# A routing stage with its scores in column lanes and its scatters spread out, and its last shared down product in the program that follows

## The chip, the cores and the metric

One NeuronCore of a Trainium2 chip runs the whole program as one launch. The metric is the device time in microseconds (us), the median of three runs. Two layers of a transformer-like network are computed on two sequences of 2048 tokens of 256 features; all of it is in float32. The change lies in the feed-forward part of the first layer, a mixture of experts.

## The reference, cut to what matters

```python
# layer 0, second half; x is [2 * 2048, 256]; h = layernorm(x) * (1 + cb) + sb
scores = h @ router                        # 256 x 8
topv, topi = top_k(scores, 2)
gates = sigmoid(scores, -inf where not chosen)
routed_e = h * gates[:, e]                 # each chosen token, times its gate
out_e = (silu(routed_e @ w_in[e]) * (routed_e @ w_swiglu[e])) @ w_out[e]
shared = (silu(h @ w_in_shared.T) * (h @ w_swiglu_shared.T)) @ w_out_shared.T
x = x + gb * (shared + sum_e out_e)
```

## The kernel before, in words

The part is two programs, one after the other, each a block in which every engine has its own hand-written order of instructions; engines wait for each other by semaphores alone. All engines of one program must have ended before any starts the next.

**route_tokens** (line 879) walks over four blocks of tokens, `it` = 0 to 3. A block is 512 tokens of each of the two sequences (`b` = 0, 1), so 1024 tokens, or eight tiles of 128. TensorE computes the shared expert for all tokens: eight projections `up(it, q)`, each into one of two buffers `ps[:, q % 2]`; ScalarE makes the silu, VectorE's `product(it, q)` multiplies and so frees the buffer for `up` two later. `down(it, b)` is the second product of the shared expert; for `b` = 1 it is made in the next block, after `up(it + 1, 1)`. VectorE scales its result (`output`), and GpSimd adds it to `x` (`add_output`); for the last block VectorE adds.

In between lies the routing. `turn` transposes the normalised rows of the next block after `up` 2 to 5. `scores(it + 1)` (line 1243) follows `down(it, 0)`: for each of eight tiles the 128 x 128 piece of `hT` is the stationary operand and the 128 x 8 router is moved through. VectorE finds the two best (`best`), marks them (`choose`: a cast, two comparisons and a sum), TensorE counts the places (`ranks`, after `up(it, 1)`), VectorE turns them to rows of a table in HBM (`place_rows`) and multiplies the tokens by their gates (`gate_rows`). GpSimd issues sixteen indirect DMAs (`scatter`) in a row that write the gated rows to HBM, and then makes four tensor operations for the next block (`modulate`: scale and shift of the rows of both sequences).

`product(it, 7)` stands behind `choose(it + 1)` in VectorE's order, and `up(it + 1, 1)` waits for `product(it, 7)`; this couples VectorE's routing work to TensorE.

**run_experts** (line 1316) takes 71 blocks of 128 rows of the table. For a block, SyncE loads the rows, TensorE transposes them (`turn`), ScalarE and VectorE copy the weights of the block's expert to a buffer (`fetch_in`, `fetch_sw`), TensorE makes `up` and `down`, and the result is stored. Its second weights, `w_out` of eight experts and of the shared one (4.7 MB), are loaded at the start by nine DMAs from GpSimd's queue (line 1358), and `down(0, 0)` waits for all of them. TensorE begins with sixteen transposes that compute nothing (`spin`), then `turn` 0 and 1, then `up` 0.

## Time and profile before

| | |
|---|---|
| median of the runs | 3204.3 us (3202.83 to 3207.18) |
| the profiled execution | 3175.27 us, of which the span of the trace is 3173.4 us |
| mean granted TensorE clock in it | 0.989 |
| TensorE matmuls, busy | 3053.4 us (96%) |
| VectorE, ScalarE, GpSimd, busy | 1954.9, 1721.0, 763.4 us |
| route_tokens on TensorE | 503 to 714 us of the span |
| run_experts on TensorE | 717 to about 1123 us |

A row of the timeline has the start in us, the time from there to the end of its last instruction, the engine, the line and operation, output and inputs, the shape of an array tile for TensorE and of the operands, the number of instructions, and in brackets the idle time ahead of it with what ended that. A float32 matmul shows as two records, each a pass of its own.

### The profile page before, as it was taken

The page shows a single profiled execution, that of the slowest core. Times are in us where ns is not written, and L with a number is a line of the kernel's source. Part 1 is how long each engine was busy: PE and PEld are TensorE (multiplying, and loading weights), DVE is VectorE, ACT ScalarE, POOL GpSimd, SP SyncE. Part 2 cuts the span into 40 slices and gives each one's busy share as a digit, 9 for nine tenths or more (in the row PEclk, how much of TensorE's full clock was granted, in tenths as well). Part 3 has the DMA queues.
Part 4 walks back from the last instruction along what each step waited for, and adds up shares of the span by engine and source line. Part 5 has one row for each costly group of instructions (what it writes and reads, how often), then busy time and mean ns, then how long its engine had stood idle before and what let it go on. Part 6 is the DMA issues. An engine that isn't in the chain of part 4 may idle for free. (4 is left out here: it accounts for less than half of the span.)

```text
span 3173.4 us, 49527 instructions
## 1 busy us (share of the span) xinstructions
PE 3053.4 (96%) x16616; PEld 1908.5 (60%) x16617; DVE 1954.9 (62%) x4607; ACT 1721.0 (54%) x3801; POOL 763.4 (24%) x1037
## 2 busy tenths in 40 slices
PE   8999998998999989999998999999999999998999
PEld 4455556558999963333334666665555666666555
DVE  6999995653333346666664787785333777777342
ACT  6776762213333326665665888875222777776221
POOL 1111113550000035555533222221011112112111
PEclk9999999999999999999999999999999999999999
DMA  9900004013111121111101000000001000000000
GB/s 330 318 1 1 1 1 165 29 54 103 46 48 48 45 77 29 31 29 26 29 14 42 10 11 9 10 8 32 1 0 36 9 11 10 9 9 5 14 14 27
DMA packets 114255, 134.11 MB, mean 42 GB/s; under 512 B 14478, under 2 KB 100342, under 8 KB 113786
## 3 DMA queue, kind: packets, MB, share of 16 engines
q1 hardware_dynamic: 106042, 109.54, 10.6%
q0 software_dynamic: 7872, 21.77, 2.2%
q8 instruction: 117, 1.92, 0.3%
q14 instruction: 96, 0.79, 0.1%
q10 hardware_dynamic: 128, 0.10, 0.0%
HBM read 60.30 MB, written 60.83 MB: 38 GB/s over the span
## 5 line engine op out<-in xcount | busy, mean ns | idle before, releaser
L1880 DVE CUSTOM_DVE_ANT_0 sb_win_masked<-ps_win_pss,sb_win_around 128x384 f32<-128x384 f32 (+1 forms) x512 | 256.3, 538 | 167.0 <-PE ps_win_pss L2008 166.9
L2320 ACT ACTIVATE sb_loc_pr<-ps_loc_psw,sb_loc_nb,sb_loc_sc 128x256 f32<-128x256 f32 x512 | 281.0, 569 | 135.9 <-DVE sb_loc_nb L2465 135.9
L2547 PE MATMUL ps_stk_banks<-sb_stk_w,sb_loc_hT 128*128 128x512 f32 x768 | 348.3, 603 | 2.7 <-ACT sb_loc_hT L2287 2.7
L1742 ACT ACTIVATE sb_win_pT<-ps_win_pst 128x512 f32<-128x512 f32 x368 | 199.8, 596 | 167.3 <-PE ps_win_pst L2019 167.2
L1473 PE MATMUL ps_exp_ps<-sb_exp_xT,sb_exp_here 128*128 128x128 f32 x2272 | 266.8, 276 | 0.0
L1473 PEld LDWEIGHTS ps_exp_ps<-sb_exp_xT,sb_exp_here 128*128 128x128 f32 x2272 | 261.0, 193 | 0.1
L2008 PE MATMUL ps_win_pss<-sb_win_kT,sb_win_q 32*128 32x384 f32 (+1 forms) x1024 | 230.4, 520 | 31.7 <-DVE sb_win_qtok L1880 21.3
L2547 PEld LDWEIGHTS ps_stk_banks<-sb_stk_w,sb_loc_hT 128*128 128x128 f32 x768 | 141.2, 190 | 177.9 <-issue 177.9
L752 PE MATMUL ps_rec_psp<-sb_rec_hT,sb_rec_w 128*128 128x512 f32 x512 | 230.1, 592 | 0.8 <-DVE sb_keep_modf L543 0.8
L2842 DVE SCALAR_TENSOR_TENSOR sb_mlp_hid<-ps_stk_banks,sb_stk_col,sb_mlp_gl 128x512 f32<-128x512 f32 (+1 forms) x112 | 75.1, 672 | 245.5 <-ACT sb_mlp_gl L2797 245.3
L2019 PE MATMUL ps_win_pst<-sb_win_qm,sb_win_kT 32*128 32x512 f32 x736 | 211.2, 647 | 1.5 <-ACT sb_win_pT L1742 1.5
L1665 POOL TENSOR_SCALAR_AFFINE_SELECT sb_win_pT<-sb_win_pT 128x512 f32<-128x512 f32 x240 | 146.5, 634 | 244.3 <-ACT sb_win_pT L1742 244.3
L2233 POOL TENSOR_TENSOR sb_loc_t<-sb_loc_t 128x512 f32<-128x512 f32 x64 | 81.4, 1272 | 468.1 <-DVE sb_loc_t L2411 468.0
L2008 PEld LDWEIGHTS ps_win_pss<-sb_win_kT,sb_win_q 32*128 32x128 f32 x1024 | 81.7, 183 | 161.2 <-DVE sb_win_qtok L1880 148.8
L2461 DVE TENSOR_REDUCE sb_loc_top<-ps_loc_psw 128x4 f32<-128x1024 f32 x128 | 156.1, 1219 | 24.9 <-PE ps_loc_psw L2585 22.4
L752 PEld LDWEIGHTS ps_rec_psp<-sb_rec_hT,sb_rec_w 128*128 128x128 f32 x512 | 96.3, 190 | 116.5 <-issue 116.5
L1637 POOL DMA_INDIRECT sb_win_got<-expert_results,sb_keep_row x64 | 61.9, 968 | 416.5 <-POOLq L1353 401.4
L2900 PE MATMUL ps_mlp_pso<-sb_stk_w,sb_mlp_hid 128*128 128x256 f32 (+1 forms) x768 | 160.5, 383 | 0.0
L1426 DVE TENSOR_TENSOR sb_exp_hid<-ps_exp_ps,sb_exp_act_f 128x512 f32<-128x512 f32 x71 | 49.1, 692 | 169.0 <-PE ps_exp_ps L1473 169.0
L2797 ACT ACTIVATE sb_mlp_gl<-ps_stk_banks,sb_stk_col 128x512 f32<-128x512 f32 x48 | 33.0, 687 | 217.1 <-PE ps_stk_banks L2889 217.0
L2900 PEld LDWEIGHTS ps_mlp_pso<-sb_stk_w,sb_mlp_hid 128*128 128x128 f32 (+1 forms) x768 | 133.1, 189 | 28.6 <-issue 10.5
L1393 ACT COPY sb_exp_xT<-ps_exp_psx 128x256 f32<-128x256 f32 x71 | 26.4, 372 | 223.8 <-PE ps_exp_psx L1464 223.8
(362 smaller groups left out, 6725.2 us busy)
## 6 DMA issues: line engine op xcount, KB each, us to landing
sorted_tokens<-sb_rec_blank SPq DMA_DIRECT2D x9, 4224.0 KB, 30.2
sb_exp_rows<-sorted_tokens SPq DMA_DIRECT2D x71, 128.0 KB, 2.0
expert_results<-sb_exp_res SPq DMA_DIRECT2D x71, 128.0 KB, 1.7
sb_moe_w_in<-in_L_ffn_w_in_eDF SPq DMA_DIRECT2D x8, 512.0 KB, 10.7
sb_moe_w_sw<-in_L_ffn_w_swiglu_eDF SPq DMA_DIRECT2D x8, 512.0 KB, 10.8
sb_exp_w_out<-in_L_ffn_w_out_eFD POOLq DMA_DIRECT2D x8, 512.0 KB, 8.7
sb_stk_angles<-in_angles SPq DMA_DIRECT2D x32, 128.0 KB, 3.8
sb_stk_xs_b<-sb_stk_y SPq DMA_DIRECT2D x64, 63.5 KB
```

What stands on the lines that cost most here:

```text
L752: i = nc.tensor.matmul(out, w[:, k, j * REC + g * P:j * REC + (g + 1) * P], hT[:, G % 2, k], start=(k == 0), stop=(k == KD - 1))
L1473: i = nc.tensor.matmul(ps[:, k % 2, j, f * P:(f + 1) * P], here[:, k % 2, j, c * FF + f * P:c * FF + (f + 1) * P], xT[:, k % 2, c], start= ...
L1665: nc.gpsimd.affine_select(part, part, [[0, AG], [-towards, P]], ALU.is_ge, outside, base=0, channel_multiplier=towards).then_inc(s_cut, 1)
L1742: nc.scalar.activation(pT[:, n % PARTS], pst[:, n % TURNED], ACT.Exp, scale=SC).then_inc(s_e, 1)
L1880: nc.vector.tensor_tensor_reduce(masked[:, pair % 2, j, 0:keys], pss[:, (n + j) % PLAIN, 0:keys], around[:, first:first + keys], 1.0, -3e3 ...
L2008: nc.tensor.matmul(pss[:, n % PLAIN, 0:len(keys) * P], q[rows, u % RINGS, g], kT[rows, keys[0]:keys[-1] + 1].rearrange("p a n -> p (a n)") ...
L2019: nc.tensor.matmul(pst[:, n % TURNED], kT[rows, key], qm[rows, u % 2].rearrange("p g n -> p (g n)"), start=True, stop=True, skip_group_che ...
L2233: nc.gpsimd.tensor_tensor(qq, qq, t2[:, 0:INNER], ALU.add).then_inc(s_rope, 1)
L2320: e = nc.scalar.activation(pr[:, hf, h], psw[:, hf, h // 2, h % 2 * 256:h % 2 * 256 + 256], ACT.Exp, scale=sc8[:, b, hh:hh + 1], bias=nb[: ...
L2461: nc.vector.tensor_reduce(top[:, hf], psw[:, hf].rearrange("p a (h n) -> p (a h) n", h=2), AX_X, ALU.max).then_inc(s_top, 1)
L2547: t = nc.tensor.matmul(psa[:, c], hT[:, b, k, 1 - k:P + 1 - k], w[:, k, c * 512:(c + 1) * 512], start=(k == 0), stop=(k == KD - 1))
L2900: i = nc.tensor.matmul(pso[:, t], hid[at:at + M, b, f, t * P:(t + 1) * P], w2[at:at + M, f], start=(f == 0 and t % 2 == 0), stop=(f == KH ...
```

## The change

The scores of a block are computed the other way round: the router, padded from 8 to 32 columns, is the stationary operand, and 256 tokens at a time are moved through; the four groups of 256 tokens use the four groups of 32 columns of the array and so 32 partitions each of one bank (`LANE`, `scores`). ScalarE copies the bank (`copy_lanes`), and two transposes (`turn_scores`) give the layout that `best` reads. The instructions lie inside `down(it, 0)`: the scores after its second quarter, the transposes after its last. `down` waits for each quarter of `hid` by itself. `ranks` comes after `up(it, 0)` instead of `up(it, 1)` (after `up(0, 2)` in the first block), and the gates on ScalarE after `silu` 0. On VectorE `place_rows` comes before `product` 1 and both `gate_rows` come before the output of the block before. In the first block `up(0, 0)` goes ahead of the transposes of the scores, and the scores no longer wait for `ones` and `before`. GpSimd's scatters go in four groups of four DMAs, and the scale, shift and add operations stand between them.

`down(3, 1)` with its scaling and addition moves from the end of route_tokens to run_experts, where it takes the place of `spin`; `hid`, `og`, the shared `w_out` and the PSUM tile are allocated across both for it. VectorE scales and adds after its first two weight copies. `up(0, 0)` there goes ahead of `turn(0, 1)`, and `silu(0, 0)` ahead of the second copy of rows. VectorE no longer waits at the end of route_tokens for the scatters to have landed; SyncE waits for them in run_experts before its first load of rows.

```diff
@@ route_tokens, GpSimd: modulate() is split in scale(it, b) and offset(it, b), scatter(it) in settle_rows(it) and scatter(pair)
                 for it in range(NBLK):
+                    settle_rows(it)
+                    scatter(0)
                     if it:
                         add_output(it - 1, 1)
-                    scatter(it)
+                    scatter(1)
                     if it + 1 < NBLK:
-                        modulate(it + 1)
+                        scale(it + 1, 0)
+                    scatter(2)
+                    if it + 1 < NBLK:
+                        offset(it + 1, 0)
+                    scatter(3)
+                    if it + 1 < NBLK:
+                        scale(it + 1, 1)
+                        offset(it + 1, 1)
                         add_output(it, 0)
@@ route_tokens, ScalarE
+                def copy_lanes(it):
+                    act.wait_ge(s_lanes, it + 1)
+                    nc.scalar.copy(lane_scores[:], psg[:, 0:2 * P]).then_inc(s_lanes_here, 1)
...
-                        if it and q == 1:
+                        if q == 0:
                             nc.scalar.preload_act_table_set(LN_SET)
                             gates(it)
@@ route_tokens, VectorE
+                product(0, 0)
                 best(0)
                 choose(0)
                 weigh(0)
+                product(0, 1)
+                for b in range(NB):
+                    scale_rows(1, b)
+                product(0, 2)
+                place_rows(0)
+                for b in range(NB):
+                    gate_rows(0, b)
 
                 for it in range(NBLK):
                     ahead = it + 1 < NBLK
-                    product(it, 0)
-                    product(it, 1)
                     if it:
+                        product(it, 0)
                         weigh(it)
-                    place_rows(it)
-                    if ahead:
+                        place_rows(it)
+                        product(it, 1)
                         for b in range(NB):
-                            scale_rows(it + 1, b)
-                    if it:
+                            gate_rows(it, b)
+                        if ahead:
+                            for b in range(NB):
+                                scale_rows(it + 1, b)
                         output(it - 1, 1)
-                    gate_rows(it, 0)
-                    product(it, 2)
-                    gate_rows(it, 1)
+                        if not ahead:
+                            table_ends()
+                        product(it, 2)
                     product(it, 3)
...
-                output(NBLK - 1, 1)
-                add_output(NBLK - 1, 1)
-                dve.wait_ge(s_sorted, NBLK * ROUTED * 16)
@@ route_tokens, TensorE
-                    for b in range(NB):
-                        pe.wait_ge(norm.s_hT, norm.ready(it, b))
-                        for n in range(TB):
-                            at = (b * TB + n) * EXP
-                            for k in range(KD):
-                                i = nc.tensor.matmul(psg[:, at:at + EXP], hT[:, it % 2, b, k, n * P:(n + 1) * P],
-                                                     router[:, k], start=(k == 0), stop=(k == KD - 1))
+                    pe.wait_ge(norm.s_hT, norm.ready(it, NB - 1))
+                    for k in range(KD):
+                        for lane in range(P // LANE):
+                            b, half = lane // HALVES, lane % HALVES
+                            i = nc.tensor.matmul(psg[lane * LANE:(lane + 1) * LANE, 0:2 * P], router[:, k],
+                                                 hT[:, it % 2, b, k, half * 2 * P:(half + 1) * 2 * P], start=(k == 0),
+                                                 stop=(k == KD - 1), skip_group_check=True)
+                    i.then_inc(s_lanes, 1)
+
+                def turn_scores(it):
+                    pe.wait_ge(s_lanes_here, it + 1)
+                    for j in range(HALVES):
+                        i = nc.tensor.transpose(psg[:, (2 + j) * P:(3 + j) * P], lane_scores[:, j * P:(j + 1) * P], ident[:])
                     i.then_inc(s_score, 1)
...
                     for f in range(KF):
+                        pe.wait_ge(s_hid, it * UF + b * KF + f + 1)
...
+                        if b == 0 and it + 1 < NBLK:
+                            if f == 1:
+                                scores(it + 1)
+                            if f == KF - 1:
+                                turn_scores(it + 1)
...
                 pe.wait_ge(s_w, 16 * 5)
+                scores(0)
+                pe.wait_ge(s_shared, 16 * 3)
+                up(0, 0)
+                turn_scores(0)
                 pe.wait_ge(s_ones, 1)
                 pe.wait_ge(s_b, 16)
-                scores(0)
-                pe.wait_ge(s_shared, 16 * 3)
                 for it in range(NBLK):
                     for q in range(UF):
-                        up(it, q)
-                        if q == 1:
+                        if it or q:
+                            up(it, q)
+                        if q == (0 if it else 2):
                             ranks(it)
-                            if it:
-                                down(it - 1, 1)
+                        if it and q == 1:
+                            down(it - 1, 1)
...
-                down(NBLK - 1, 1)
@@ run_experts, SyncE, VectorE, TensorE
+                sp.wait_ge(s_sorted, NB * NBLK * TB * 2 * 16)
                 for n in range(UNROLL):
                     load(0, n)
...
                 fetch_sw(0, 0)
                 fetch_sw(0, 1)
+                late_output()
                 product(0, 0)
...
-                spin(nc, ident, psw, 16)
+                for f in range(KF):
+                    late_down(f)
                 turn(0, 0)
+                up(0, 0)
                 turn(0, 1)
-                up(0, 0)
```

## Rows read from the trace of the kernel before

**Rows 1.** The page, busy time of each engine over the span.
```profile
PE 3053.4 (96%) x16616; PEld 1908.5 (60%) x16617; DVE 1954.9 (62%) x4607; ACT 1721.0 (54%) x3801; POOL 763.4 (24%) x1037
```
**Rows 2.** Waits of TensorE, 500 to 720: total us, times, longest.
```profile
PE ps_route_ps L1260 <- DVE sb_route_hid L1166: 7.4, 3, 3.9
```
**Rows 3.** Timeline, start of route_tokens.
```profile
506.48 0.47 SPq L949 DMA_DIRECT2D sb_route_w_out<-in_shared_out  x1
...
510.07 5.38 PE L1250 MATMUL ps_route_psg<-sb_route_router,sb_route_hT 128*128 128x8 f32 x32 [2.40 <-issue]
...
515.30 3.62 PE L1260 MATMUL ps_route_ps<-sb_route_hT,sb_moe_w_in 128*128 128x512 f32 x4
```
**Rows 4.** DMA issues, 500 to 740: count, KB, median us to landing.
```profile
sb_route_w_out<-in_shared_out SPq DMA_DIRECT2D x1, 512.0 KB, 6.4
sb_exp_w_out<-in_shared_out POOLq DMA_DIRECT2D x1, 512.0 KB, 13.1
```
**Rows 5.** Timeline of TensorE, scores(1) and the projections behind them.
```profile
547.37 3.63 PE L1250 MATMUL ps_route_psg<-sb_route_router,sb_route_hT 128*128 128x8 f32 x32
550.86 1.96 PE L1260 MATMUL ps_route_ps<-sb_route_hT,sb_moe_w_in 128*128 128x512 f32 x4
...
554.37 1.88 PE L1260 MATMUL ps_route_ps<-sb_route_hT,sb_moe_w_in 128*128 128x512 f32 x4
```
**Rows 6.** Timeline of TensorE: up(1, 1), ranks(1), and up(1, 6) behind scores(2).
```profile
565.33 2.73 PE L1260 MATMUL ps_route_ps<-sb_route_hT,sb_moe_w_in 128*128 128x512 f32 x4 [3.92 <-DVE sb_route_hid L1166]
...
570.56 0.19 PE L1267 MATMUL ps_route_psg<-sb_route_chosen,sb_route_before 128*128 128x64 bf16 x1
...
603.85 3.66 PE L1260 MATMUL ps_route_ps<-sb_route_hT,sb_moe_w_in 128*128 128x512 f32 x4
```
**Rows 7.** Windows, TensorE: stretch, length, busy, granted clock, DMA share, GB/s.
```profile
565.30:568.70 3.40, 3.37 (x5) 0.67 0.00 0
603.80:607.20 3.40, 3.40 (x6) 0.53 0.22 78
```
**Rows 8.** Timeline of VectorE, the two comparisons of choose(0) and of choose(1).
```profile
517.88 0.36 DVE L1118 TENSOR_TENSOR sb_route_pick<-sb_route_number,sb_route_topf 128x64 f32<-128x64 f32 x2
...
557.53 4.72 DVE L1118 TENSOR_TENSOR sb_route_pick<-sb_route_number,sb_route_topf 128x64 f32<-128x64 f32 x2
```
**Rows 9.** Timeline of GpSimd: block 0's last scatter, a scale, the slowest scatter.
```profile
554.09 0.96 POOL L976 DMA_INDIRECT sorted_tokens<-sb_route_gated,sb_route_rowu  x1 [0.30 <-issue]
...
559.82 2.35 POOL L964 TENSOR_TENSOR sb_route_xn<-sb_route_xn,sb_layer_moe_scale_row 128x1024 f32<-128x1024 f32 x1
...
700.61 1.44 POOL L976 DMA_INDIRECT sorted_tokens<-sb_route_gated,sb_route_rowu  x1 [0.30 <-issue]
```
**Rows 10.** Timeline of TensorE, four products in 32-column tiles in a later stage.
```profile
1186.08 1.06 PE L2044 MATMUL ps_win_pso<-sb_win_pT,sb_win_v 128*32 128x512 f32 x8
```
**Rows 11.** Timeline, end of route_tokens.
```profile
706.16 0.69 DVE L1166 TENSOR_TENSOR sb_route_hid<-ps_route_ps,sb_route_act_f 128x512 f32<-128x512 f32 x1 [2.74 <-ACT sb_route_act_f L1013]
...
706.91 7.17 PE L1285 MATMUL ps_route_pso<-sb_route_w_out,sb_route_hid 128*128 128x256 f32 x32 [1.41 <-DVE sb_route_hid L1166]
...
715.38 1.22 DVE L1179 TENSOR_TENSOR sb_keep_x<-sb_keep_x,sb_route_og 128x1024 f32<-128x1024 f32 x1
```
**Rows 12.** Timeline, start of run_experts.
```profile
717.25 3.29 PE L116 MATMUL ps_exp_psw<-sb_keep_ident 128*128 128x128 f32 x16 [3.16 <-PEq L939]
...
722.71 0.44 PE L1464 MATMUL ps_exp_psx<-sb_keep_ident,sb_exp_rows 128*128 128x128 f32 x2 [2.18 <-DMA sb_exp_rows<-sorted_tokens]
...
723.81 0.75 POOL L1358 DMA_DIRECT2D sb_exp_w_out<-in_shared_out  x1
726.64 0.69 PE L1464 MATMUL ps_exp_psx<-sb_keep_ident,sb_exp_rows 128*128 128x128 f32 x2 [3.49 <-DMA sb_exp_rows<-sorted_tokens]
...
732.41 3.74 PE L1473 MATMUL ps_exp_ps<-sb_exp_xT,sb_exp_here 128*128 128x128 f32 x32
...
737.09 1.99 PE L1487 MATMUL ps_exp_pso<-sb_exp_w_out,sb_exp_hid 128*128 x8 [0.94 <-DVE sb_exp_hid L1426]
```

105 lines of the change are left out of this document (65 added, 40 removed).

## The prediction, made before the changed kernel was run

> **What bounds the kernel now.** Read the page's busy times first: TensorE works 96% of the span [rows 1], so a change in this stage pays what it takes from TensorE's own line of work, and nothing that it takes from another engine. Then read TensorE's waits in 500 to 720: in all the routing stage it waits for VectorE's product three times, 7.4 us together, the longest 3.9 [rows 2]. Next its timeline: the start, where the scores run from 510.07 and the first projection follows at 515.30 [rows 3]; a block, where the scores take 550.86 - 547.37 = 3.49 us and a projection 554.37 - 550.86 = 3.51 [rows 5] (3.43 where nothing precedes it but another); and the two places where passes run slower: up(1, 1) behind the 3.92 us wait takes 570.56 - 565.33 = 5.23 us, and the first four passes of up(1, 6), straight behind the scores, 3.66 instead of 1.88 [rows 6]. The windows show why: the granted clock was 0.67 and 0.53 there [rows 7], a stretch with time at the lower level, 1.2 instead of 2.4 GHz. Before the one the engine was idle for 3.92 us; before the other it made the thirty-two narrow passes. Last, the end: the last projection's product begins at 706.16, the last down product at 706.91, and two operations of VectorE end the program at 715.38 + 1.22 = 716.6 [rows 11]; the experts' program starts at 717.25, gets its first rows at 722.71 and its second at 726.64, and makes its first down product at 737.09 [rows 12].
>
> **The change, part by part.** All sums are made against the profiled execution (3175.27 us), which is 29.0 us below the median of the runs; I take the difference between the kernels to be the same in both.
>
> *Start.* up(0, 0) no longer follows the old scores. It waits for three shared weights; the last of them is issued at 506.48 and takes 6.4 us to land [rows 3, 4], so 512.9. The new scores lie ahead of that: they start after the affine of the rows, near 509, and are 16 passes. So the first projection starts at 512.9 instead of 515.30: 2.4 us. The cost of its first half at the lower clock (3.62 us for four passes [rows 3]) stays.
>
> *Scores of blocks 1 to 3.* Sixteen passes of 256 columns in four column tiles replace thirty-two. The nearest row is of the same tile shape: eight passes of 512 columns in 1.06 us [rows 10], so four tiles do work side by side. Counted by columns the new ones take 1.0 us, counted by passes 2.1; without any overlap 3.4 (a projection's pass of 512 columns takes 3.43 / 8 = 0.43 us, one of 256 half of it, sixteen times). I take 1.5, since the row is of this form, and 0.3 for the two transposes, below the 0.44 that two take with their end [rows 12]. ScalarE's copy between them hides under two quarters of the down product (3.5 us). So 3.49 - 1.8 = 1.7 us a block, 5.1 in three; the bounds are a loss of 0.6 (three times 3.4 + 0.3 against 3.49) and a gain of 6.6 (1.0 + 0.3).
>
> Eight passes of 0.43 us on four tiles would take 0.86; the row shows 1.06 [rows 10], so 0.2 us is all that entering and leaving the narrow tiles can have cost there. The Trainium skill (TensorEngine Tiling (Array Packing), Key Properties) says that changing the tiling mode drains TensorE; by that rule each scoring inside a down product pays two such changes, which at 0.2 us for each is 1.2 us in three blocks off the sum; it moves no rival.
>
> *TensorE's waits for product(it, 7).* VectorE's two comparisons take 0.36 us in choose(0), but 4.72 in choose(1), when GpSimd runs its scale and shift, 2.35 us each [rows 8, 9]: each comparison ends with a GpSimd operation. I put the whole of the 7.4 us down to that. In the new order the scores are ready at the end of down(it, 0), 3.5 us earlier, and ranks ask for `chosen` after up(it, 0), 3.4 us earlier; the two cancel. What moves is GpSimd: gate_rows now start after product 1 and end 14 us into a block (up(it, 0) 3.4, silu and two table loads to 8.9, two times 2.2), so its queue runs from 14.5: sixteen scatters at 0.96 + 0.30 = 1.26 us, 20.2, and six operations of 2.35, 14.1 [rows 9], to 49 in a block of 45.8 (eight projections 27.4, two down products 13.9, turns 1.8, ranks 0.8, scores 1.8). choose runs from 44 and meets the last three operations (42 to 49), so it ends 3.3 into the next block; ranks ask at 3.4, product 7 ends at 4.0, up 1 asks at 4.2. So nothing is left of the wait where the queue starts on time. In block 1 it doesn't: its gate_rows meet the first block's addition and end 2.1 us later; that leaves 1.8 us. Gain 7.4 - 1.8 = 5.6. The bounds: with two more collisions a block (2.35 each) the waits stay as they are, 0; with none, 7.4.
>
> *The lower clock.* If the 3.92 us wait and the thirty-two narrow passes go, so do their costs: 5.23 - 3.43 = 1.8 us and 3.66 - 1.88 = 1.8 us [rows 6, 7]. The wait that I leave, 1.8 us, is nearer to the idle 1.41 us behind which the down product ran at full speed (7.17 us for 32 passes [rows 11]) than to the 3.92. Gain 3.6; bounds 0 and 3.6.
>
> *The turn in block 0.* VectorE's place_rows now follow the scaling of the rows, so the 0.4 us wait of the first turn goes.
>
> *End.* Before, the program ended 716.6 - 706.85 = 9.75 us after the last product of a projection [rows 11]: down(3, 1) and two operations of 1.22 us. They go to run_experts. GpSimd's last scatter is issued 37 us into a block of 42, five before the end; so SyncE's new wait for the scatters, behind which all loads of rows are queued, costs nothing. The price of the moved part: down(0, 0) there waits for nine loads of w_out, the last issued at 723.81, landing 13.1 us later at 736.9 [rows 4, 12]; TensorE was ready at 732.41 + 3.74 = 736.15. So this start is bound by 4.7 MB of weights: 737.09 - 717.25 = 19.8 us from the start. New order on TensorE from its start: 7.0 for the moved product; turn(0, 0), whose rows land at 5.5, 0.4; copy 0.6; up(0, 0) 3.7; turn 1, whose rows land at 9.4, and its copy, 1.2; up(0, 1) 3.7: 16.6 us, 3.2 below 19.8. Even if the moved product's first half ran at the lower clock (3.5 more) the end would move by 0.3 us only. Gone with `spin` is nothing that counts. VectorE's two operations lie between its weight copies and product(0, 0), which waits until 11 us. So all 9.75 us are gained. An idle time of 3.2 us ahead of down(0, 0) may bring the lower clock; a step there costs up to 1.8 us, I take 1.
>
> Sum: 2.4 + 5.1 + 5.6 + 3.6 + 0.4 + 9.75 - 1.0 = 25.9 us. I round down to 25 for small waits of the new order: the profiled execution at 3150.3 us, the median at 3204.3 - 25 = **3179.3 us**.
>
> **The rivals.** *The collisions stay.* For it: every GpSimd operation but one still runs while VectorE casts, compares or scales, and the margins above are a few tenths. Against: only three of the six still lie near choose. Then the waits (5.6) and the wait's clock (1.8) aren't gained: 25 - 7.4 = 17.6, so 3186.7 us. The Trainium skill (SBUF — State Buffer, the diagram's notes on the shared port pair) says that a VectorE operation with two inputs in SBUF and a GpSimd operation that reads SBUF exclude each other, each for its whole length. That is the rule under the 4.72 us; the trace agrees (0.36 against 4.72).
>
> *The experts' start doesn't hide it.* If the weights were not the limit but the rows' loads or TensorE's own order, of the 9.75 us the moved product's 7.0 would come back on TensorE: 25 - 7 = 18, 3186.3 us. Against it stands the landing at 736.9.
>
> *The change does little.* The scores gain nothing (no overlap of the tiles), collisions stay, and the moved product comes back: 25 - 5.7 - 7.4 - 7 = 4.9, so 3199.4 us. It needs all three.
>
> *Slower: GpSimd's queue sets the pace.* From gated(it) over sixteen scatters and six operations to the shift that the next gate_rows wait for is a ring: 14.1 - 2.35 + 20.2 + 4.4 + 1 = 37 us against a block of 45.8. One scatter took 1.44 us instead of 0.96 [rows 9]. VectorE's scaling and statistics now lie beside scatters. From an issue of 1.26 + 8.8 / 16 = 1.8 us the ring decides; at 3.5 us it is 37 + 16 x 2.24 = 73, three blocks cost 3 x 27 = 81 us and the kernel is 81 - 25 = 56 us slower, 3260; it is slower at all from about 2.4 us. Sixty-three of the 64 issues show 0.96 to 1.05 and stood partly beside the same VectorE work.
>
> **How the numbers follow.** The forecast has 0.66, with its own range from 19.3 (tiles without overlap, 5.7 less) to 28 (neither the wait of 1.8 nor the clock's 1.0): 3176 to 3185. Collisions that stay 0.15, an experts' start that doesn't hide it 0.08, both among 3184 to 3189; little 0.07; slower 0.04. The range that should hold 8 in 10 goes from 3174 (28 us and a run-to-run spread of 2) to 3192 (collisions that stay and tiles without overlap, 25 - 7.4 - 5.7 = 12 us). Under 0.2% (6.4 us) a measurement of this kernel can't tell a difference from none; faster by more 0.90, within 0.06, slower 0.04.
>
> **What would show it.** In the changed profile: the first projection at about 513; the scores as 16 passes in 1 to 2 us inside the down product; no wait for product 7 over 2 us, and no window of the stage after 520 with a clock under 0.9; route_tokens ending about 26.5 us earlier on TensorE's start of the experts (717.25 to about 691); down(0, 0) 19.8 us behind that start, with the idle time ahead of it. Wrong would be the sum if VectorE's comparisons again take 4 us with TensorE waiting, if the column tiles run one behind the other, or if down(0, 0) comes later than 20.5 us behind its start.

## The result, and the profile of the changed kernel

The changed kernel took 3166.32 us (median, 3165.41 to 3166.53), the kernel before 3205.16 us (3202.83 to 3207.18): a ratio of 0.9875, 95% interval 0.9859 to 0.989, so 38.8 us less where the forecast was 25 and the range ended at 3174. The two profiled executions tell another size: spans of 3173.4 and 3164.8 us, 8.6 us apart. That contradiction is the real question of this case, and the runs below answer most of it.

First the trace of the changed kernel against the steps of the prediction. Waits of TensorE, 500 to 720, the answer to [rows 2] (total us, times, longest):

```profile
PE ps_exp_pso L1544 <- DMA sb_exp_w_out<-in_shared_out: 4.4, 1, 4.4
PE ps_route_ps L1299 <- DMA sb_moe_shared_out<-in_shared_out: 3.2, 1, 3.2
PE ps_route_psg L1306 <- DVE sb_route_chosen L1151: 2.3, 1, 2.3
...
PE ps_route_pst L1272 <- DVE sb_route_xn L1119: 1.4, 1, 1.4
```

The wait for product 7 is gone; what is left of it is one wait of `ranks` for `chosen` (2.3) and a new one of a turn for rows that VectorE normalises (1.4). TensorE's timeline, where [rows 3], [rows 5] and [rows 6] stood:

```profile
510.15 1.07 PE L1282 MATMUL ps_route_psg<-sb_route_hT,sb_route_router 128*32 128x256 f32 x16 [1.19 <-ACT sb_route_hT L1023]
514.38 3.78 PE L1299 MATMUL ps_route_ps<-sb_route_hT,sb_moe_w_in 128*128 128x512 f32 x4 [3.16 <-DMA sb_moe_shared_out<-in_shared_out]
517.95 3.12 PE L1299 MATMUL ps_route_ps<-sb_route_hT,sb_moe_w_sw 128*128 128x512 f32 x4
...
540.50 3.62 PE L1324 MATMUL ps_moe_pso<-sb_moe_shared_out,sb_route_hid 128*128 128x256 f32 x16
544.05 1.07 PE L1282 MATMUL ps_route_psg<-sb_route_hT,sb_route_router 128*32 128x256 f32 x16
545.05 3.72 PE L1324 MATMUL ps_moe_pso<-sb_moe_shared_out,sb_route_hid 128*128 128x256 f32 x16
548.61 0.38 PE L1290 MATMUL ps_route_psg<-sb_keep_ident,sb_route_lane_scores 128*128 128x128 f32 x2
548.82 1.88 PE L1299 MATMUL ps_route_ps<-sb_route_hT,sb_moe_w_in 128*128 128x512 f32 x4
...
563.05 7.07 PE L1324 MATMUL ps_moe_pso<-sb_moe_shared_out,sb_moe_late_hid 128*128 128x256 f32 x32
569.96 1.88 PE L1299 MATMUL ps_route_ps<-sb_route_hT,sb_moe_w_in 128*128 128x512 f32 x4
...
608.19 0.20 PE L1306 MATMUL ps_route_psg<-sb_route_chosen,sb_route_before 128*128 128x64 bf16 x1 [2.32 <-DVE sb_route_chosen L1151]
```

The scores of a block take 545.05 - 544.05 = 1.00 us and their transposes 548.82 - 548.61 = 0.21. The down product around them takes 3.55 + 3.56 = 7.11 us in its two halves, an undivided one 569.96 - 563.05 = 6.91; so the scores cost 1.00 + 0.21 + 0.20 = 1.41 us a block instead of 3.49. The whole of up(0, 0) ran at the lower clock, 6.53 us (514.38 to 520.91). The windows of TensorE for it, for up(2, 1) behind the wait for `chosen`, and for down(0, 0) of the experts, to be read as [rows 7]:

```profile
514.40:520.90 6.50, 6.50 (x8) 0.53 1.05 407
608.80:612.30 3.50, 3.50 (x5) 0.56 0.00 0
716.00:720.00 4.00, 4.00 (x11) 0.50 0.00 0
```

The end, the answer to [rows 11, 12]:

```profile
691.67 1.88 PE L1299 MATMUL ps_route_ps<-sb_route_hT,sb_moe_w_sw 128*128 128x512 f32 x4
695.23 7.14 PE L1551 MATMUL ps_moe_pso<-sb_moe_shared_out,sb_moe_late_hid 128*128 128x256 f32 x32 [1.68 <-PEq L947]
702.21 0.38 PE L1521 MATMUL ps_exp_psx<-sb_keep_ident,sb_exp_rows 128*128 128x128 f32 x2
...
707.91 3.74 PE L1530 MATMUL ps_exp_ps<-sb_exp_xT,sb_exp_here 128*128 128x128 f32 x32
716.00 3.77 PE L1544 MATMUL ps_exp_pso<-sb_exp_w_out,sb_exp_hid 128*128 x8 [4.36 <-DMA sb_exp_w_out<-in_shared_out]
```

The rows are there when the moved product is done (no wait at 702.21), and down(0, 0) waits for the weights, 20.8 us behind the program's first matmul, as before (19.8). VectorE and GpSimd around that wait for `chosen`, the answer to [rows 8, 9]:

```profile
603.17 4.70 DVE L1147 TENSOR_TENSOR sb_route_pick<-sb_route_number,sb_route_topf 128x64 f32<-128x64 f32 x2
...
603.15 2.34 POOL L976 TENSOR_TENSOR sb_route_xn<-sb_route_xn,sb_layer_moe_shift_row 128x1024 f32<-128x1024 f32 x1
605.46 2.34 POOL L994 TENSOR_TENSOR sb_keep_x<-sb_keep_x,sb_route_og 128x1024 f32<-128x1024 f32 x1
```

The last down product of the experts starts at 1120.51 before and 1102.24 after: 18.3 us, or 19.6 counted from the spin at the start of route_tokens (503.38 and 504.67). So this pair of executions has the gain that the prediction's mechanism gives, less some us, and then loses 11 us of it in the windowed attention (583.7 us before, 594.9 after; another execution of the kernel before has 590.3). It doesn't have 38.8.

### The profile page after: what moved, and what is told of

Its sections match the earlier page's. It is cut to its first block and busy times, and to the rows that moved or that the text cites. A ratio compares the mean times of both kernels' runs of the same rounds, so it can differ in the third digit from the quotient of the medians.

```text
span 3164.8 us, 49386 instructions
## 1 busy us (share of the span) xinstructions
PE 3051.6 (96%) x16544; PEld 1895.5 (60%) x16545; DVE 1947.1 (62%) x4607; ACT 1725.4 (55%) x3807; POOL 764.8 (24%) x1037
## 5 line engine op out<-in xcount | busy, mean ns | idle before, releaser
L2074 PE MATMUL ps_win_pss<-sb_win_kT,sb_win_q 32*128 32x384 f32 (+1 forms) x1024 | 233.9, 528 | 31.2 <-DVE sb_win_qtok L1946 20.5
L2966 PEld LDWEIGHTS ps_mlp_pso<-sb_stk_w,sb_mlp_hid 128*128 128x128 f32 (+1 forms) x768 | 133.1, 189 | 28.6 <-issue 10.5
```

The lines of the kernel that those rows point to most:

```text
L2074: nc.tensor.matmul(pss[:, n % PLAIN, 0:len(keys) * P], q[rows, u % RINGS, g], kT[rows, keys[0]:keys[-1] + 1].rearrange("p a n -> p (a n)") ...
L2966: i = nc.tensor.matmul(pso[:, t], hid[at:at + M, b, f, t * P:(t + 1) * P], w2[at:at + M, f], start=(f == 0 and t % 2 == 0), stop=(f == KH ...
```

## The experiments

Every job shows the kernel before beside its own runs. A chip is named by a number; each job ran on one. In this section "the spin" is the row of transposes on TensorE with which route_tokens begins, the common zero of two traces. "remote" in a row stands where the profile names no engine and no DMA as what ended a wait.

**Both kernels again.** No edit.

> The kernel before, unchanged, on the chip of these runs. My theory: the gain of the routing stage and of the experts' start is 21 us at the experts' first down product (737.09 to 716.0), 18 us at the experts' end; the rest of the difference between the two measured gaps (8.6 us between the profiled executions, 38.8 us between the medians) comes from the windowed attention or a later stage of the kernel before, which has more than one duration. It expects executions of this kernel that differ by up to 29 us with the routing stage alike within 2 us, and the difference all behind 1125 us. The rival: the slower executions are slower in the routing stage itself (collisions of GpSimd and VectorE that fall otherwise), and then the gain there is above 21 us.

> The changed kernel, unchanged, beside it. Theory: 3166 us, all its executions within 2 us of one another, the experts' first down product at 716 us, and the windowed attention from 1107 to about 1702 us. The rival (each kernel has several durations of the later stages by chance of the chip): some execution near 3195 or near 3156.

Chip 14: the kernel before 3178.19 us (19 runs, 3172.28 to 3184.82), itself as an experiment 3176.56 (ratio 0.9993), the changed one 3156.73 (ratio 0.9927, 0.991 to 0.9943): 21.5 us. The changed kernel is 10 us faster than its first time, the kernel before 27 us. So it is mainly the kernel before that has two levels: a first near 3205 to 3209 us, and one near 3178. In the routing its two traces are alike within 2 us, as expected (the last projection starts 200.2 and 198.6 us behind the spin). The executions of the changed kernel, expected within 2 us of 3166, lie from 3152.76 to 3165.53: there the rival held.

**The parts alone.** Routing only puts the old end back:

```diff
-                dve.wait_ge(s_x, (NBLK - 1) * NB)
-                dve.wait_ge(s_last, 1)
+                output(NBLK - 1, 1)
+                add_output(NBLK - 1, 1)
+                dve.wait_ge(s_sorted, NBLK * ROUTED * 16)
+                dve.wait_ge(s_x, (NBLK - 1) * NB)
+                dve.wait_ge(s_last, NB)
...
+                down(NBLK - 1, 1)
```

> The routing change alone; the last down product with scaling and addition stays at the end of route_tokens, and run_experts is as before, with its spin. Theory: the experts' program starts 12 to 14 us earlier than before (near 704), and its first down product comes 19.8 us behind that. If the later stages keep their durations, 12 to 14 us faster than before. The rival, that the windowed attention's duration hangs on when it starts, expects another offset of up to 30 us either way that arises behind the experts.

Late product only is the kernel before with the changed run_experts:

```diff
-                down(NBLK - 1, 1)
...
+                for f in range(KF):
+                    late_down(f)
```

> The moved down product alone, with the new start of run_experts; the routing of the kernel before. Theory: the experts' program starts 9.7 us earlier (near 707.5), its first down product 19.8 to 21 us behind that; 8 to 10 us faster at that place. If the moved product were not hidden there: 2 to 3 us. The rival on the later stages again expects an offset that arises behind the experts.

Chip 14: 3164.15 us (0.995, 0.9934 to 0.9967), 14.0 us less, as expected, and 3175.94 (0.9995, 0.9986 to 1.0005), 2.3 less, which isn't clear of noise, where 8 to 10 were expected. Alone, the moved product gains almost nothing. TensorE and GpSimd of that kernel:

```profile
706.31 0.96 POOL L979 DMA_INDIRECT sorted_tokens<-sb_route_gated,sb_route_rowu  x1 [0.30 <-issue]
...
712.93 9.11 PE L1506 MATMUL ps_moe_pso<-sb_moe_shared_out,sb_moe_late_hid 128*128 128x256 f32 x32 [7.27 <-PEq L942]
...
713.38 6.12 POOL L1358 DMA_DIRECT2D sb_exp_w_out<-in_L_ffn_w_out_eFD  x8 [6.11 <-POOLq L942]
```

GpSimd's last indexed write is done at 707.3, yet the next program starts 5.7 us later on TensorE and 6.1 later on GpSimd. In the changed kernel the last write is issued in full at 688.2, 5.4 us before TensorE is through with the program (693.55), and the start at 695.23 waits for little. So the move pays in full only because the new order has the last write issued before TensorE is done (14.0 + 2.3 against 21.5 together).

**The new scores alone**, in the kernel before.

```diff
-        router = m.sb("router", [P, KD, EXP])
+        router = m.sb("router", [P, KD, LANE])
+        lane_scores = m.sb("lane_scores", [P, 2 * P])
...
                                 scores(it + 1)
+                                turn_scores(it + 1)
```

> The kernel before with the scores in column lanes alone (scores, copy and transposes right behind down(it, 0), all else as before). Theory: the sixteen passes and two transposes take 1.2 us of TensorE instead of 3.5, the copy between them is no longer hidden (about 0.8 us more of waiting), so 1.5 us a block, and the lower clock of up(1, 6), which I put down to the thirty-two narrow passes, is gone (1.8 us). 5 to 6 us earlier at the end of route_tokens; the three waits for product 7 stay at 1 to 4 us each. The rival (the waits for VectorE have the same root as the clock) expects the waits to go too: 12 us.

Chip 11: 3172.85 us against 3178.98 (0.9989, 0.9974 to 1.0005): not clear of noise by the times. In the trace the last projection starts 194.7 us behind the spin, where the kernel before has 200.2 and 198.6 in two traces: about 4 to 5.5 us less. The three waits for product 7 are all there (0.79, 4.19, 4.16 us), so the passes and the waits are separate gains.

**GpSimd's order**, two ways, in the changed kernel: the writes in one row, or the second modulation ahead of the last four writes.

```diff
-                    scatter(0)
+                    for pair in range(4):
+                        scatter(pair)
                     if it:
                         add_output(it - 1, 1)
-                    scatter(1)
...
```

> The changed kernel with GpSimd's sixteen scatters in one row again, its tensor operations behind them (the addition of the block before first). Theory: what counts is only that the last operations of GpSimd meet choose; their end stays 34.3 us behind gated rows, so TensorE's waits stay within 1 us of those of the changed kernel (2.3 us for chosen in block 2, with 1.8 us of lower clock behind it), route_tokens as long within 2 us. The rival, that spreading the scatters is what frees VectorE, expects 5 us or more longer.

```diff
+                        scale(it + 1, 1)
+                        offset(it + 1, 1)
                     scatter(3)
-                    if it + 1 < NBLK:
-                        scale(it + 1, 1)
-                        offset(it + 1, 1)
+                        pool.wait_ge(s_chosen, it + 2)
```

> The changed kernel with GpSimd's three operations of sequence 1 ahead of the last four scatters, and the addition of sequence 0 held until chosen is there. Theory: choose meets no GpSimd operation that holds it for long; comparisons at 0.36 us; the wait for chosen in block 2 (2.3 us) and the lower clock behind it (1.8 us) vanish: route_tokens ends 4 us earlier than in the changed kernel. The rival (the lower clock comes by chance of the moment, not from the wait) expects 2.3 us at most.

**The idle time ahead of the experts' first down product covered**, in the changed kernel.

```diff
+                        pe.wait_ge(s_late_og, 1)
+                        spin(nc, ident, late_pso[:, 0], 34)
                         pe.wait_ge(s_wo, 16 * (EXP + 1))
```

> The changed kernel with 34 transposes that compute nothing between up(0, 1) and down(0, 0) of run_experts, where TensorE waits 4.4 us for the last weights. Theory: the wait is for the weights, so down(0, 0) stays at 20.8 us behind the start, and without an idle time the first down product takes 1.99 instead of 3.77 us and the up behind it 3.74 instead of 4.61: 2.8 us less to the end of the experts. If the weights were not the limit down(0, 0) would come later by the transposes' 3.7 us.

Chip 11: 3152.83 us (0.9909, 0.9889 to 0.9928), 3152.82 (0.9914, 0.9896 to 0.9932) and 3152.4 (0.9914, 0.9897 to 0.9932). The changed kernel itself didn't run on this chip; on two others it took 3156.7 and 3156.6, so the gain of about 4 us is one between jobs. The row of writes was expected to make no difference, and its trace has no wait for `chosen` at all: the last projection starts 181.3 us behind the spin, where the changed kernel has 186.8 to 187.0 in three traces and 183.3 and 183.5 in two others, so 2 to 5.7 us sooner. In the changed kernel it is the interleaving that puts an addition beside VectorE's comparisons. The other order moves the wait (1.61 us, in block 1, at full clock behind it; 182.7). The transposes of the third kernel give down(0, 0) its clock back; the row above them is its wait for `chosen`:

```profile
606.77 0.20 PE L1306 MATMUL ps_route_psg<-sb_route_chosen,sb_route_before 128*128 128x64 bf16 x1 [2.30 <-DVE sb_route_chosen L1151]
...
708.36 3.88 PE L119 MATMUL ps_moe_pso<-sb_keep_ident 128*128 128x128 f32 x34
712.66 1.99 PE L1546 MATMUL ps_exp_pso<-sb_exp_w_out,sb_exp_hid 128*128 x8 [0.42 <-DMA sb_exp_w_out<-in_shared_out]
```

1.99 us instead of 3.77, and from down(0, 0) to the last one 383.4 us instead of 386.2, as the kernel before has it (383.4). It has the same instructions as the changed kernel up to there, and still its last projection came 3.5 us sooner behind the spin (183.5): the waits are alike, 2.30 and 1.42 us, but up(2, 1) ran at full clock, as its window shows:

```profile
607.40:610.90 3.50, 3.50 (x8) 1.00 0.00 0
```

That much two executions of one program differ.

**Both kernels cut short.** Up to here my theory was that the executions of a kernel part only in the windowed attention, with the clock that each is granted there. Leaving stages out tells whether they do. The edit is one line, in both kernels, with stages=(1, 2, 3) for the other pair:

```diff
-    build_program(nc, aps)
+    build_program(nc, aps, stages=(1, 2))
```

> Leaves out the windowed attention and the local layers: the kernel before, cut behind the experts, whose rows are stored and not added (x is written out as the recurrence left it). Last experts' down product of the full kernel before: 1120.5 us of the span, so some 1125 to 1160 us with the stores and the output. Theory (the executions of one kernel part only behind the experts, in the windowed attention, with its granted clock): the executions of this cut kernel lie within 3 us of each other, where those of the full one lie 12 to 17 us apart. Rival (they part in the recurrence, the routing or the experts): they lie apart by more than 6 us, and the granted clock of the stages goes with it.

> Leaves out the windowed attention and the local layers: the changed kernel, cut at the same place. Theory: 18 to 20 us below the cut kernel before (last down product at 1102.2 and 1120.5, with spins at 504.7 and 503.4), executions within 3 us of each other; the forecast's 25 us would need the whole of the end's 9.75 and of the waits. Rival (the 38.8 us of the first measurement are the change's own work): more than 25 us, up to 39.

> Leaves out the local layers: the kernel before cut behind the windowed attention. Spin of that stage at 1125.3 and 583.7 us of windowed attention: near 1715 to 1740 us with the output. Theory: the executions lie 6 to 14 us apart, nearly as far as those of the full kernel (12 to 17), longer where the granted clock is lower. Rival (the local layers spread them): within 3 us.

> Leaves out the local layers: the changed kernel cut behind the windowed attention. Theory: its median 10 to 20 us below the cut kernel before, less exactly than with two stages, since each execution draws its clock in the windowed attention; no fixed share of 39 us. Rival (the earlier end of the experts makes the windowed attention itself shorter for a fixed reason): the difference is over 30 us in every pair of executions.

This job ran on chip 7, where the kernel before took 3207.17 us (3200.03 to 3213.14), so the first level again. Two stages: 1160.33 and 1118.67 us, 41.7 apart where my theory had 18 to 20, executions within 5 us. Three stages: 1754.09 and 1715.01, 39.1 apart. The whole of the 38.8 us lies in the first two stages: there my theory fell and its rival held. Executions do spread more with the windowed attention (8.4 and 10.6 us against 4.9 and 3.2), as the theory said, but the difference of the kernels doesn't arise there. The cut kernel before has what the profile ahead of the prediction does not show. TensorE, scores(2):

```profile
602.12 2.23 PE L1250 MATMUL ps_route_psg<-sb_route_router,sb_route_hT 128*128 128x8 f32 x18
604.68 0.17 PE L1250 MATMUL ps_route_psg<-sb_route_router,sb_route_hT 128*128 128x8 f32 x1 [0.33 <-issue]
606.08 0.40 PE L1250 MATMUL ps_route_psg<-sb_route_router,sb_route_hT 128*128 128x8 f32 x2 [1.23 <-issue]
606.81 0.38 PE L1250 MATMUL ps_route_psg<-sb_route_router,sb_route_hT 128*128 128x8 f32 x1 [0.34 <-issue]
608.90 0.17 PE L1250 MATMUL ps_route_psg<-sb_route_router,sb_route_hT 128*128 128x8 f32 x1 [1.71 <-issue]
...
612.14 3.58 PE L1260 MATMUL ps_route_ps<-sb_route_hT,sb_moe_w_in 128*128 128x512 f32 x4
```

612.14 - 602.12 = 10.0 us for what takes 3.49 in [rows 5]; the other blocks 7.4 and 9.0. No wait on a semaphore explains the gaps ("issue"). In the same time VectorE stands before its scaling of the down product, which TensorE finished at 602.1, and GpSimd issues indexed writes; the rows of both:

```profile
607.50 0.96 POOL L976 DMA_INDIRECT sorted_tokens<-sb_route_gated,sb_route_rowu  x1 [0.30 <-issue]
...
611.10 1.23 DVE L1173 TENSOR_TENSOR sb_route_og<-ps_route_pso,sb_keep_gates 128x1024 f32<-128x1024 f32 x1 [14.80 <-remote]
```

VectorE starts 2.6 us behind the end of the last of sixteen writes, 9 us late (its wait in the kernel's profile ahead of the prediction was 6.0 us, here 14.8). The same comes in all four blocks, at 552.82, 611.10, 664.95 and 717.84: 3.1 us before, 2.6 and 1.2 behind and 0.3 before the end of the last write, after waits of 10.5, 14.8, 13.4 and 8.2 us (6.0, 6.0, 6.0 and 0.6 in the profile ahead of the prediction). What is handed on during the first six writes isn't late: VectorE's product at 591.73 follows right behind ScalarE's end at 591.70. The one at the end holds back the last product: 26.3 us from the last projection to the experts' first turn instead of 19.1, and 10.6 us are lost before it. TensorE of the cut changed kernel on the same chip loses nothing of the kind: its last projection is 187.0 us behind the spin, as in the changed kernel's first profile.

Two smaller marks of it are there all the same. Only in blocks 1 and 2 does the changed kernel have four groups of four writes. In block 0 nothing stands between the first two groups, so eight are in a row, and in block 3, where there is nothing left to scale, twelve. Behind the eight ScalarE's copy comes 2.2 us late, and at the twelve VectorE's scaling 1.5 us, in the changed kernel's first profile as in the cut one (546.64 and 687.58). The rows of the first profile, and then the same two of the changed kernel on chip 14:

```profile
547.35 0.37 ACT L1039 COPY sb_route_lane_scores<-ps_route_psg 128x256 f32<-128x256 f32 x1 [5.82 <-remote]
688.31 1.23 DVE L1202 TENSOR_TENSOR sb_route_og<-ps_moe_pso,sb_keep_gates 128x1024 f32<-128x1024 f32 x1 [2.30 <-remote]
...
544.18 0.37 ACT L1039 COPY sb_route_lane_scores<-ps_route_psg 128x256 f32<-128x256 f32 x1 [3.66 <-PE ps_route_psg L1282]
685.76 1.23 DVE L1202 TENSOR_TENSOR sb_route_og<-ps_moe_pso,sb_keep_gates 128x1024 f32<-128x1024 f32 x1 [0.77 <-PE ps_moe_pso L1324]
```

So the changed kernel was profiled where this hold-up exists, and the profile ahead of the prediction shows none of it. That is why the two profiled spans are only 8.6 us apart: they belong to different levels.

**Which part of the change removes it.** Three partial kernels and a changed kind of write, all cut behind the experts.

> The kernel before with the new scores alone, cut behind the experts like the other two-stage kernels (windowed attention and local layers left out). The cut kernel before took 1160.3 us and the cut changed kernel 1118.7 where the full kernel before took 3207 us. Theory (in such executions TensorE gets the 64 short passes of a score block late while GpSimd issues its 16 indexed writes: 7.4, 10.0 and 9.0 us a block instead of 3.5): the 16 passes take 1.1 us a block, without idle time between them, so 3 x (9 - 1) = 24 us less and 1 to 8 us more with TensorE's clock behind them: 1128 to 1138 us. Rival (the writes hold up VectorE's and ScalarE's work as much as TensorE's, and the number of passes matters little): no more than 10 us less, 1150 to 1157. Where the full kernel before takes 3178 us instead, nothing waits and both theories expect 5 us less than a cut kernel before of some 1137 us.

> The kernel before with only the late down product moved into the experts' program, cut the same way. Theory: the score blocks still take 7 to 10 us each; only the end gains, from 4 us (as in the full kernel on a quicker occasion) to 12 us, where the last product and VectorE's work before it came 8 us late: 1148 to 1156 us. Rival (the late end is the larger part of what is lost): under 1140 us.

> The changed kernel with GpSimd's 16 indexed writes in one row again instead of spread between the modulation, cut the same way. Theory (few passes are enough): 5 us under the cut changed kernel's 1118.7, as far as the full kernel showed, so 1113 to 1116 us. Rival (spreading the writes is what keeps the other engines supplied): VectorE's scaling of the product and TensorE's passes come 4 to 10 us late again behind the writes, and the time is over 1125 us.

> The kernel before, cut the same way, with the 64 indexed writes of the token rows replaced by 64 plain writes of the same size to fixed places, issued by GpSimd as well (leaves out the sorting: the experts then read rows in token order and blank ones). Theory (GpSimd's building of the indexed writes' descriptors is what holds the others up): the 64 short passes of a score block take 3.5 us in every block and VectorE scales the product at its end, 1130 to 1140 us even where the kernel with indexed writes takes 1160. Rival (the bytes on the DMA rings hold up the supply, whatever kind of write carries them, or that chip's TensorE is late for another reason): the blocks stay at 7 to 10 us, 1155 to 1162 us.

The edit of the last one:

```diff
-                            pool.indirect_dma_start(t["sorted"], bass.IndirectOffsetOnAxis(ap=rowu[:, n, c:c + 1], axis=0),
-                                                    gated[:, n, c], None).then_inc(s_sorted, 16)
+                            slot = ((it * TI + n) * 2 + c) * P
+                            pool.dma_start(t["sorted"][slot:slot + P], gated[:, n, c]).then_inc(s_sorted, 16)
```

Chip 6, where the kernel before took 3208.86 us (3200.26 to 3215.5). The two kernels to compare with were cut on chip 7, where it took 3207.17, so the differences between the two chips' rows are good to a few us. Last projection counted from the spin:

| two stages only (chip 6, or 7 where named) | median us | last projection |
|---|---|---|
| kernel before (chip 7) | 1160.33 | 210.9 |
| new scores alone | 1162.76 | 211.6 |
| late product alone | 1151.46 | 217.8 |
| changed kernel, writes in one row | 1137.91 | 201.4 |
| changed kernel (chip 7) | 1118.67 | 187.0 |
| kernel before, plain writes | 1139.04 | 196.6 |

The new scores alone gain nothing there, against my expectation of 22 to 32 us, and lie outside the rival's range too. Their trace says why. ScalarE, VectorE and TensorE in block 2:

```profile
602.90 1.07 PE L1262 MATMUL ps_route_psg<-sb_route_hT,sb_route_router 128*32 128x256 f32 x16
...
611.88 1.22 DVE L1186 TENSOR_TENSOR sb_route_og<-ps_route_pso,sb_keep_gates 128x1024 f32<-128x1024 f32 x1 [14.90 <-remote]
...
612.04 0.37 ACT L1022 COPY sb_route_lane_scores<-ps_route_psg 128x256 f32<-128x256 f32 x1 [15.12 <-remote]
...
612.47 0.69 PE L1270 MATMUL ps_route_psg<-sb_keep_ident,sb_route_lane_scores 128*128 128x128 f32 x2 [8.50 <-ACT sb_route_lane_scores L1022]
```

TensorE is through with its 16 passes at once, but two engines that wait for different things of TensorE (the product at 602.9, the scores at 604.0) both go on only at 611.9 and 612.0; the last write of this block is issued at 608.15. It isn't the number of passes: an engine that needs something of another one late in a row of sixteen writes (what is handed on in the first six isn't late) gets it near the row's end, VectorE between 3.1 us before and 2.8 behind the last write, ScalarE 2.6 to 2.9 behind. The late product alone gains 8.9 us, as expected, though its last projection comes later still.

With plain writes in their place (16 issued in 8.6 us instead of 20.0) VectorE waits 6.0 us again and the score blocks take 3.5 to 4.0 us: 21.3 us less than the kernel before, within what my theory expected.

```profile
600.91 1.22 DVE L1173 TENSOR_TENSOR sb_route_og<-ps_route_pso,sb_keep_gates 128x1024 f32<-128x1024 f32 x1 [6.02 <-PE ps_route_pso L1285]
```

Whether it is the kind of write or the shorter row that helps, this run doesn't separate. A part of the 21.3 is another gain: the last projection comes 2 to 3.6 us sooner than in the kernel before without any hold-up (198.6 and 200.2). And the writes back in one row cost the changed kernel 19.2 us here, where I had expected a gain of 3 to 6 and the rival a loss; on chip 11 they gained 2 to 5.7 us of the trace.

**A better version, and the changed kernel beside it.** The order of the second GpSimd experiment and the transposes together, since both keep the writes spread.

> The changed kernel with two edits together: GpSimd's modulation of the second sequence stands ahead of the last four indexed writes, and 34 transposes stand on TensorE before the experts' first down product. Each alone gave 3152.8 and 3152.4 us where the kernel before took 3179.0. Theory (the indexed writes hold the other engines up only where many stand in a row, and here they still stand in three groups): 2 to 6 us below the changed kernel in this call, whether the kernel before takes 3178 or 3207 us. Rival (8 writes in a row at the end are enough to hold others up): as fast as the changed kernel or slower where the kernel before takes 3207 us.

> The changed kernel itself, beside it. Theory (its own time hardly depends on the chip, since its writes are spread, and the time of the kernel before does): 3153 to 3167 us whatever the kernel before takes; the ratio 0.987 where that takes 3207 us and 0.993 where it takes 3178. Rival (both kernels move together with the chip): the ratio is the same 0.990 at either level.

Chip 5, the kernel before 3178.33 us (3167.99 to 3190.26): 3149.9 (0.9911, 0.989 to 0.9933) and 3156.57 (0.9936, 0.9915 to 0.9958). The second ratio is the 0.993 that was expected at this level, and not the rival's 0.990. The intervals overlap, so 6.7 us less is likely and not shown. It wasn't run on a chip of the other level.

## Why the prediction was wrong

**The step that failed** is the sentence under the parts: the profiled execution "is 29.0 us below the median of the runs; I take the difference between the kernels to be the same in both". The 29 us were not a constant of measuring that both kernels share. From chips 14 and 5 to the first measurement the kernel before goes up by 27 us and the changed one by 10, so 17 us of the gap belong to the kernel before alone. Its two traces place them in the very stage that the change edits: 17.8 us up to the experts' first turn (10.6 in the routing, 7.2 behind it), lost on chips where a row of indexed writes holds up the other engines; the profile ahead of the prediction came from an execution without that. Where the kernel before takes 3178 us, the change gains 21.5 and 21.8 us, near the 25 of the sum (partly by luck, as its terms come to 19.2 below); 21.5 + 17.8 = 39.3 is about what it gains where that takes 3205 to 3207 (38.8 measured, and 41.7 in two stages). The price that was left out is that of the row of writes, an operation whose cost the trace at hand could not show on the engines that pay it.

**The edit costed as nearly free**, spreading the writes, is the one that pays there: about 19 of the 41.7 us, the one read on chip 6 and the other on chip 7. The prediction looked at GpSimd's order only for its collisions with VectorE. The rival *GpSimd's queue sets the pace* asked whether spread writes could cost more; that a row of them costs was in no rival. "Sixty-three of the 64 issues show 0.96 to 1.05" stays nearly true on those chips too (all 0.96 to 1.09 us in the cut kernel before): the issuing engine shows nothing, those that wait do.

**The sum, term by term**, on the two profiled executions:

| term | predicted | measured |
|---|---|---|
| start | 2.4 | 2.2 (11.92 to 9.71 behind the spin) |
| its first half at the lower clock | 0 | -1.4 (6.53 against 5.17 us) |
| scores | 5.1 | 6.2 (three times 3.49 - 1.41) |
| waits in the blocks | 5.6 | 3.7 (7.4 to 2.3 + 1.4) |
| lower clock in the blocks | 3.6 | 1.8 (up(2, 1), 5.23 us, has it again) |
| turn in block 0 | 0.4 | 0.4 |
| end | 9.75 | 9.1 (last projection to down(0, 0), 33.5 to 24.3) |
| clock behind the idle time there | -1.0 | -2.8 |
| sum | 25.9 | 19.2 |

The mechanisms were right. The column tiles do run side by side (1.00 us, where columns said 1.0 and the bound 3.4), less than the 1.5 taken from eight passes of twice the width [rows 10]. The Trainium skill (TensorEngine Tiling (Array Packing), Key Properties) states that a change of the tiling mode drains TensorE. The trace agrees as far as it goes: the divided down product is 0.20 us longer than the undivided one, and the sixteen passes take 1.00 us where their columns need 0.86 (sixteen times half of 0.43, four side by side), so the two changes cost 0.34 us at most, near the 0.2 each that the prediction had. The wait that was left, 2.3 us, was foreseen for block 1 and came in block 2: two of GpSimd's operations (603.15 and 605.46) beside VectorE's two comparisons, 4.70 us again. A wait of 1.8 us was held too short for the lower clock: 2.32 us brought it in one execution and 2.30 not in another. The experts' start was limited by the weights, as argued: 20.8 us instead of 19.8. Its start came 22.0 us earlier (23.3 counted from the spin), not 26.5, which is the shortfall of the routing. Of the signs of being wrong that were named beforehand three came: the comparisons took 4.70 us with TensorE waiting, down(0, 0) came 20.8 us behind its start instead of at most 20.5, and a window behind 520 had a clock of 0.56. All three make the gain smaller, so they don't carry the miss.

Not in the sum at all: that the moved product pays only together with the earlier writes (2.3 us alone). "GpSimd's last scatter is issued 37 us into a block of 42, five before the end" was the right sentence, but as a reason for no cost, not as the condition of the gain.

**Open.** What passes between the engines late, the semaphore or the next instructions, isn't told: TensorE's gaps with no wait speak for instructions, the common restart of VectorE and ScalarE fits both; no packet of a queue of instructions shows in the cut kernel between 600 and 612, so a late load of them isn't seen. Whether it is the kind of write or the length of the row isn't separated. Why chips 6 and 7 have it and 5, 11 and 14 don't isn't known. The changed kernel too was 10 us slower in the first measurement than on chips 5 and 14 (3166.3 against 3156.6 and 3156.7). Between the first profile and that of chip 5 the routing holds 3.5 us of it and the windowed attention 11.7 (594.9 against 583.2); but the profile on chip 14 has 593.4 there too, so it isn't the chip's level alone, and the cause stays open.

## What to carry to other kernels

When the profiled execution and the timed ones differ by more than the change is worth, find out where before using either: the gap may be the very stage that is edited. Cutting both kernels behind the edited stage settles in one job what whole kernels leave to guesses. Put other work between indexed writes of GpSimd (no more than four in a row here left no mark on others), and look at the engines that wait while they are issued, not at GpSimd, for their price.

## What was not expected of the hardware

- On two of the five numbered chips, a row of sixteen indexed writes (20 us) keeps VectorE from going on until 3.1 us before to 2.8 behind its end (waits of 8.2 to 14.9 us instead of 0.6 to 6.0) and ScalarE until 2.6 to 2.9 behind it, and TensorE's 32 matmuls of 8 columns take 7.4 to 10.0 us instead of 3.5. Sixteen plain writes of the same rows don't. Rows of eight and twelve in the changed kernel make another engine 1.5 to 2.2 us late; of groups of four with 2.4 us of arithmetic between them nothing is seen.
- TensorE began the next program 5.7 us after GpSimd's last indexed write was issued in full, with its own part done before 705.7 us and the start at 712.93.
- The clock behind an idle time isn't fixed by the idle time: 2.32 and 2.30 us at the same instruction, 0.56 granted behind the one and full speed behind the other.
